# State-space layer: the scan's output copied out of PSUM by ScalarE and multiplied by the gate on GpSimd

## The reference

```python
xz = hidden_states @ in_proj_w.T
x, z = jnp.split(xz, 2, axis=-1)
...
x = silu(jnp.transpose(xc, (0, 2, 1)))          # xc: x after a convolution of 4 taps
A = -jnp.exp(A_log)
dt, Bm, C = jnp.split(x @ x_proj_w.T, [DT_RANK, DT_RANK + D_STATE], axis=-1)
dt = jax.nn.softplus(dt @ dt_proj_w.T + dt_proj_b)
def step(h, ins):
    h = jnp.exp(dt_t[:, :, None] * A) * h + dt_t[:, :, None] * B_t[:, None, :] * x_t[:, :, None]
    y = jnp.einsum('bdn,bn->bd', h, C_t)
    return (h, y)
...
y = jnp.transpose(ys, (1, 0, 2)) + x * D
return y * silu(z) @ out_proj_w.T
```

## Time and profile before

| | |
|---|---|
| median of three executions | 3272.32 us |
| the three | 3270.14, 3272.32, 3275.80 us |
| the profiled execution | 3271.81 us |
| its span in the trace | 3270.1 us |
| mean granted clock of TensorE in the span | 0.919 of full speed |

### The profile page before, as it was taken

How to read it: one execution, slowest core, us unless ns; L and a number is a source line. 1 busy time by engine, 2 the same in 40 slices (tenths; PEclk the granted TensorE clock), 3 DMA queues, 4 the chain that set the end, 5 groups by cost and what they waited for, 6 DMA issues and landing times.

```text
span 3270.1 us, 45199 instructions
## 1 busy us (share of the span) xinstructions
PE 2865.6 (88%) x14018; PEld 1320.2 (40%) x14055; DVE 2167.0 (66%) x3006; ACT 1420.8 (43%) x2463; POOL 1267.8 (39%) x1424
## 2 busy tenths in 40 slices
PE   6895798988988989869999999678899899999986
PEld 5662133333332333236666666563222233223222
DVE  3577876866866767022222222564999999999997
ACT  2341055655655656812122211435445445545442
POOL 1143012112212212210000000744888888898885
PEclk9997588988999989979999999888899999998978
DMA  6166413133132220041111111740000000000000
GB/s 206 52 213 161 152 28 61 28 59 55 34 58 38 51 48 24 19 135 32 32 30 32 32 31 26 224 152 7 1 14 20 1 20 20 1 20 14 1 13 20
DMA packets 175061, 176.60 MB, mean 54 GB/s; under 512 B 50674, under 2 KB 151541, under 8 KB 174749
## 3 DMA queue, kind: packets, MB, share of 16 engines
q1 hardware_dynamic: 168732, 157.52, 18.9%
q0 software_dynamic: 6144, 16.82, 1.6%
HBM read 100.46 MB, written 73.83 MB: 53 GB/s over the span
## 4 chain that ended last, share of the span: by engine, by line
PE 54%; DVE 18%; POOL 10%; issue 9%; ACT 4%; DMA 3%; SPq 1%; POOLq 0%; DVEq 0%; ACTq 0%; PEldq 0%
PE ps L1679 50%; DVE hh L1645 6%; DVE mp L1421 6%; POOL Ch L907 5%; DVE ps L1632 2%; PE ps L1887 2%; POOL yg L806 2%; DMA ks<-qk_parts 1%; ACT Pt L1029 1%; DVE tl L1622 1%; DVE q L1333 1%; SPq L529 1%; PE ps L1843 1%; SPq L620 1%; ACT dA L1209 1%
## 5 line engine op out<-in xcount | busy, mean ns | idle before, releaser
L1421 DVE TENSOR_REDUCE mp<-ps 128x1 f32<-128x1024 f32 (+7 forms) x768 | 669.4, 909 | 245.3 <-PE ps L1679 234.2
L1029 ACT ACTIVATE Pt<-ps 128x512 f32<-128x512 f32 (+3 forms) x1280 | 609.2, 539 | 477.3 <-PE ps L1679 472.2
L907 POOL TENSOR_TENSOR Ch<-hh,Cb 128x1024 f32<-128x1024 f32 x256 | 603.1, 2358 | 41.0 <-DVE hh L1645 41.0
L1679 PE MATMUL ps<-ks,qs 96*128 96x512 bf16 (+3 forms) x1280 | 392.0, 379 | 96.2 <-DVE mp L1421 48.6
L1645 DVE TENSOR_TENSOR_SCAN hh<-dA,hst,ps 128x512 f32<-128x512 f32 x384 | 472.8, 1262 | 0.0
L767 POOL TENSOR_SCALAR_AFFINE_SELECT Pt<-Pt 128x128 f32<-128x128 f32 x512 | 146.8, 292 | 837.1 <-ACT Pt L1029 828.6
L1679 PE MATMUL ps<-qs,ks 99*128 99x512 bf16 (+3 forms) x1280 | 406.9, 365 | 16.0 <-ACT Pt L1029 15.6
L1209 ACT ACTIVATE dA<-ps 128x1024 f32<-128x1024 f32 x256 | 261.8, 1023 | 356.2 <-PE ps L1679 355.8
L1679 PE MATMUL ps<-dtx,pick 32*128 32x512 f32 x1024 | 324.8, 685 | 74.0 <-DVE hh L1645 73.1
L1632 DVE TENSOR_TENSOR ps<-ps,Bb 128x512 f32<-128x512 f32 x512 | 325.4, 680 | 28.0 <-PE ps L1679 27.7
L1679 PE MATMUL ps<-dt,WA 32*128 32x512 f32 x1024 | 321.1, 706 | 15.6 <-ACT dA L1209 14.6
(11 more groups left out here) (303 smaller groups left out, 3770.5 us busy)
## 6 DMA issues: line engine op xcount, KB each, us to landing
W<-in_L_ffn_w SPq DMA_DIRECT2D x16, 1024.0 KB, 12.1
qk_parts<-q SPq DMA_DIRECT2D x32, 384.0 KB, 2.9
qs<-qk_parts SPq DMA_DIRECT2D x96, 128.0 KB, 6.1
ks<-qk_parts SPq DMA_DIRECT2D x96, 128.0 KB, 7.8
expert_out<-yb SPq DMA_DIRECT2D x72, 128.5 KB, 2.6
expert_in<-zero SPq DMA_DIRECT2D x9, 1024.0 KB, 11.5
xg<-expert_in SPq DMA_DIRECT2D x72, 128.0 KB, 2.7
X<-in_L_attn_x SPq DMA_DIRECT2D x4, 1024.0 KB, 9.7
```

Source lines behind the costliest of these rows:

```text
L907: pool.tensor_tensor(Ch[:, k % 6, :, :], hh[:, k % HRING, :, :], Cb[:, par:par + 1, :].broadcast_to([P, 2, CH]), ALU.mult).then_inc(s_Ch, 1)
L1029: act.activation(Pt[:, n % PRING, q0:CH], ps[:, 4 + n % SRING, q0:CH], ACT.Exp, scale=SCALE).then_inc(s_exp, 1)
L1421: dve.tensor_reduce(mp[:, qc, h, t % TPC, k0 // 1024:k0 // 1024 + 1], slot[:, 0:n], AX.X, ALU.max).then_inc(s_free, 1)
L1679: return pe.matmul(o, lhsT, rhs, start=start, stop=stop, **kw)
```

## The change

`gate_y` leaves VectorE. ScalarE gets `take_y`, which copies bank 6 into a new SBUF tile `yv` (one buffer of 128 x 512), at units 10, 18 and 26 and at unit 2 of the next chunk, right behind that unit's `decay`. GpSimd gets `gate_y`, which multiplies `yv` by `zs` into `zs`, at units 11, 19 and 26 and at unit 2 of the next chunk, right behind that unit's `Ch`. `reduce` of the next block now waits for the copy (`s_yev`) and not for the gate, and `take_y` waits for the gate before it, since `yv` has one buffer. The last block's pair stands behind the loop.

```diff
--- before.py
+++ after.py
@@ -402,6 +402,7 @@
         hh = sb("hh", [P, HRING, 2, CH])
         Ch = sb("Ch", [P, 6, 2, CH])
         ob = sb("ob", [P, 2, CH])
+        yv = sb("yv", [P, CH])
         xo = sb("xo", [P, TPC, D])
 
         s_phase = sem("s_phase")
...
@@ -875,6 +876,12 @@
                 pool.wait_ge(s_xs, m + 1)
                 pool.tensor_tensor(dtx[:, par, d, :], dt[:, par, d, :], xs[:, par, d, :], ALU.mult).then_inc(s_dtx, 1)
 
+            def gate_y(n, d):
+
+                pool.wait_ge(s_yev, n * KI + d + 1)
+                pool.wait_ge(s_zs, n + 1)
+                pool.tensor_tensor(zs[:, n % 2, d, :], yv[:, :], zs[:, n % 2, d, :], ALU.mult).then_inc(s_yz, 1)
+
             def add(n, a):
 
                 pool.wait_ge(s_jfree, JOB[f"o{a}", n] + 1)
@@ -914,8 +921,13 @@
                     series(n + 1, 2, 0)
                 if n and u in (1, 3, 5):
                     series(n, (2, 3, 3)[u // 2], (1, 0, 1)[u // 2])
+                if u in (11, 19, 26):
+                    gate_y(n, (11, 19, 26).index(u))
+                if n and u == 2:
+                    gate_y(n - 1, KI - 1)
                 if n and u in (17, 30):
                     add(n - 1, u // 30)
+            gate_y(NC - 1, KI - 1)
             add(NC - 1, 0)
             add(NC - 1, 1)
             stage_end(pool, 6)
@@ -1200,6 +1212,12 @@
                 if n:
                     act.wait_ge(s_sum, 2 * n + a - 1)
                 act.activation(ob[:, a, :], ps[:, BANK[f"o{a}", n], :], ACT.Copy).then_inc(s_jfree, 1)
+
+            def take_y(n, d):
+                act.wait_ge(s_red, (n * KI + d) * 4 + 4)
+                if n or d:
+                    act.wait_ge(s_yz, n * KI + d)
+                act.activation(yv[:, :], ps[:, 6, :], ACT.Copy).then_inc(s_yev, 1)
 
             def decay(k):
 
@@ -1230,6 +1248,10 @@
                 n, u = divmod(k, UNITS)
                 if k + ARING < NC * UNITS:
                     decay(k + ARING)
+                if u in (10, 18, 26):
+                    take_y(n, u // 8 - 1)
+                if n and u == 2:
+                    take_y(n - 1, KI - 1)
                 if n and u in (15, 27):
                     take_o(n - 1, u // 27)
                 if n == 0 and u in (3, 7, 11):
@@ -1260,6 +1282,7 @@
                     take_z(n + 1, u - 28)
                 if u == 31:
                     silu_z(n + 1)
+            take_y(NC - 1, KI - 1)
             take_o(NC - 1, 0)
             take_o(NC - 1, 1)
             stage_end(act, 6)
@@ -1647,12 +1670,6 @@
                 if a:
                     ins.then_inc(s_h, 1)
 
-            def gate_y(n, d):
-
-                dve.wait_ge(s_red, (n * KI + d) * 4 + 4)
-                dve.wait_ge(s_zs, n + 1)
-                dve.tensor_tensor(zs[:, n % 2, d, :], ps[:, 6, :], zs[:, n % 2, d, :], ALU.mult).then_inc(s_yz, 1)
-
             select(0, 0)
             for k in range(NC * UNITS):
                 n, u = divmod(k, UNITS)
@@ -1664,12 +1681,7 @@
                     select(n + 1, 0)
                 if n and u in (0, 4, 8):
                     select(n, u // 4 + 1)
-                if u in (11, 19, 27):
-                    gate_y(n, u // 8 - 1)
-                if n and u == 3:
-                    gate_y(n - 1, KI - 1)
                 scan(k, 1)
-            gate_y(NC - 1, KI - 1)
             stage_end(dve, 6)
 
 
@@ -2064,8 +2076,9 @@
             def reduce(p):
 
                 n, par, d, i, hf = unit_of(2 * p)
+                if i == 0 and p:
+                    pe.wait_ge(s_yev, p // 4)
                 if i == 0:
-                    pe.wait_ge(s_yz, p // 4)
                     mm(ps[:, 6, :], Dd[:, d, :], xs[:, par, d, :], True, False)
                 pe.wait_ge(s_Ch, 2 * p + 2)
                 for j in range(4):
```

More of the change, by code:

```diff
@@ L446, in build @@
         s_jfull, s_jfree = sem("s_jfull"), sem("s_jfree")
-        s_xs, s_zs, s_ln, s_poly, s_mask, s_sel, s_dt, s_dtx = (sem(n) for n in ("s_xs", "s_zs", "s_ln", "s_poly", "s_mask", "s_sel", "s_dt", "s_dtx"))
+        s_xs, s_zs, s_ln, s_poly, s_mask, s_sel, s_dt, s_dtx, s_yev = (sem(n) for n in ("s_xs", "s_zs", "s_ln", "s_poly", "s_mask", "s_sel", "s_dt", "s_dtx", "s_yev"))
         s_dtb, s_dxb, s_dA, s_Bu, s_h, s_hst, s_Ch, s_red, s_yz, s_sum = (sem(n) for n in ("s_dtb", "s_dxb", "s_dA", "s_Bu", "s_h", "s_hst", "s_Ch", "s_red", "s_yz", "s_sum"))
```

## The result

The changed kernel takes 3282.2 us in the median of 15 executions (3272.95 to 3287.21), the kernel before 3272.32 us (15 executions). The ratio is 1.0031, with a 95% interval of 1.0023 to 1.0039: 9.9 us slower, 10 us by the ratio. The forecast was 3280, slower.

What follows compares the result with a forecast made beforehand. VectorE, 97% busy in the state-space loop, was taken as full, with GpSimd lacking slack at some chunk boundaries. 16.3 lost, 9.9 gained and 1.3 lost in the tail gave 7.7 us longer: 3280 us, range 3258 to 3295.

Steps and rivals of the forecast that it cites:

- Direction and place: Whole program: 7.7 us longer, with loss at chunk boundaries and in the tail, gain at units 11 and 19.
- The signs named: GpSimd waits before unit 26's gate, some 20 us; VectorE's mask wait grows 5.7 to some 30; TensorE's waits move under 7.7.
- The late copy: Unit 26: GpSimd stands waiting for ScalarE's queued copy, delaying its later work by 0.9 to 5.1 us at seven boundaries.
- The boundaries: Seven chunk boundaries: GpSimd's delay plus 1.22 us, less slack, makes masks and selects late, 16.3 us lost together.
- The port: Selects on VectorE beside GpSimd's instructions: taken as 0 us longer, with 32 us as the far bound.
- Rival (f): Selects lengthened by the port: half of the 32 us on top of the sum, 3296 us; chance 0.05.
- Units 11 and 19: Inside chunks, GpSimd has room; VectorE gains 0.58 us each, 9.9 us with the last chunk's unit 27.
- The tail: Behind the loop, copy, GpSimd multiplication and one more handover replace the last gate: 1.3 us lost.
- the sum of 7.7 us: Whole program: 16.3 lost at boundaries, 9.9 gained, 1.3 lost in the tail, so 7.7 us longer.
- (b): Loop: GpSimd's 134 free us swallow all and VectorE gains, 16.7 us after the tail: 3256 us; chance 0.13.
- (d): TensorE catches up while VectorE waits, mostly beside unit 27; some 10 us come back: 3270 us; chance 0.16.
- (e): Boundaries have no slack anywhere, as late masks hold ScalarE and its decay: 24.3 us longer, 3297 us; chance 0.12.

Runs made afterwards that it cites:

- e2: Against the kernel before, only the gates of blocks 2 and 3 (units 26 and 2, and the tail's) move to GpSimd: 1.0090, 29.9 us slower.
- e1: Against the kernel before, only the gates of blocks 0 and 1 (units 11 and 19) move to GpSimd: 0.9944, 18.6 us faster.
- e10: The changed kernel timed again on another chip, against the kernel before: 1.0012.
- e3: The changed kernel with ScalarE's copy of block 2 issued at unit 25, ahead of take_dt: 0.9973 against the kernel before, 9.0 us faster.
- e4: All gates on GpSimd, those of blocks 2 and 3 at the next chunk's units 11 and 12, with the earlier copy: 0.9942 against the kernel before.
- e9: e7 plus GpSimd waiting at unit 26 for ScalarE's copy, multiplying nothing; gates on VectorE: 1.0016 against the kernel before.
- e6: The kernel before plus an unused 128x512 multiplication on GpSimd at units 11 and 19: 0.9986, 4.6 us faster.
- e5: The kernel before plus an unused 128x512 multiplication on GpSimd at units 26 and 2: 1.0010, 3 us slower.
- e7: The kernel before plus unused 128x512 copies on ScalarE at units 10, 18, 26 and the next chunk's unit 2: 1.0010.
- e8: e4 with the very last gate done by VectorE straight from PSUM: 0.9919 against the kernel before, 26.9 us faster.

## Why the prediction was right, step by step

**Direction and place: right, shown.** The loss sits at units 26 to 8, in the half that e2 moves, and the gain in the half that e1 moves. The selects wait longer in the one and not in the other. That the chain is GpSimd's series, ScalarE's mask, VectorE's select is shown by the rows above.

**The signs named: kept.** GpSimd waits for the copy at unit 26 (at six boundaries of seven), the selects wait longer, and in this trace VectorE's wait for TensorE moved by 4.2 us in the loop, less than the 7.7 at stake; in e10's it moved by more.

**The late copy: right, and its size right only in sum.** At 1-2 I had GpSimd standing 2.9 us and it was 5.2; at 0-1 2.7 and it was none; at 3-4 some 1.3 and it was 4.1; in all it was 24.0 us, and the same reading of the trace before had given 21.4. That the sum came out is in part luck. At 1-2 VectorE itself waits 2.96 us for TensorE beside it, which it did not before. e3 shows that this step decides the sign: with the copy early 9 us faster, with it late 4 to 10 us slower.

**The boundaries: undersized.** From unit 24 of a chunk to unit 9 of the next the seven came to -1.6, 7.1, 1.8, 5.7, 3.7, 2.5 and 2.4 us against before, 21.6 in all, where I had 16.3. The excess is at the three that had no slack: 16.5 us against 9.5. Two things are in it: the longer stand at unit 26 and the selects.

**The port: the term that failed.** I took 0 for longer selects; they are 8 us longer in all. The Trainium skill's rule (SBUF — State Buffer, "Who interferes with whom"), that one of the two engines waits for the other's whole instruction, fits: in this trace all selects but the first begin while GpSimd has an instruction under way, and each ends 0.6 us behind the end of that instruction. So its length is set by when it starts. A select that has to wait for its mask often starts just after `series` ends, where a product of 2.36 us has begun on GpSimd: the seven of unit 8 take 2.1 to 2.3 us (the one at 2539.41 is among them), and took 2.2 to 2.7 before. After the change nine of the fourteen at units 0 and 4 take 2.1 to 2.3 us too, where three took about as long before, and these two units make up 7.1 of the 8 us. The moved gate itself was the instruction under way for six selects of unit 28; these take 7.8 us where they took 6.0. So the longer selects come mostly from when the select starts and only in a small part from the gate: e1 and e4, with 16 and 32 gates on GpSimd at other units, have shorter ones than before (45.3 and 46.0 us), and e9, with no gate there, has 61.4 us. Rival (f) had the right mechanism at twice the size (16 us), and the term left out cost 8.

**Units 11 and 19: right at seven chunks, undersized at chunk 0.** Between units 9 and 24 chunks 1 to 7 became 10.2 us shorter in all, 1.2 us each in most cases (two gates, as priced), 2.4 and 1.7 in chunks 1 and 4. Chunk 0 became 6.2 us shorter, 62.6 to 56.4. This is so in all kernels that move blocks 0 and 1 (56.3 to 56.4 on three chips) and in none that doesn't, except e6 (57.3). Two parts of it can be read. The select of unit 13 and the product beside it, in the timeline of the kernel before:

```profile
2308.63 2.34 POOL L907 TENSOR_TENSOR Ch<-hh,Cb 128x1024 f32<-128x1024 f32 x1
...
2308.96 2.60 DVE L1622 COPY_PREDICATED tl<-te,dtx 128x512 f32<-128x512 int32 x1
```

and in that of the kernel after, where it starts ahead of the gate on GpSimd and that is the one to be stretched (1.74 and not 1.27 us):

```profile
2307.30 0.81 DVE L1645 COPY_PREDICATED tl<-te,dtx 128x512 f32<-128x512 int32 x1
...
2307.45 1.74 POOL L883 TENSOR_TENSOR zs<-yv,zs 128x512 f32<-128x512 f32 x1
```

That is 1.8 us. Further, between units 9 and 24 TensorE's granted clock was at its lower level (half of full) for 17.1 us before, in two stretches of 3.4 and 13.7, and for 6.8 us after, and VectorE's waits there fell from 4.3 to 1.6 us: 2.7 us. The same 17.1 us stand in the traces of e2, e5, e7 and e9, the same 6.8 in those of e1, e3, e4, e8 and e10, and 10.2 us in that of e6. That the clock is the cause was not tried.

**The tail: right in kind.** 1.3 predicted; from the end of the last `reduce` to the output it is 2.15 us and was 0.91, 1.2 us more. The lower clock, in that `reduce` and in the output's multiplications, took the other 1.5 us, and no term stood for it.

**So the sum of 7.7 us against 6.1 in the traced span and 10 in the medians hides errors that cancelled, which is luck:** the boundaries lost 21.6 and not 16.3, the stretches off the boundaries won 17.0 and not 9.9 (chunk 0 alone 6.2 and not 1.2), the tail lost 2.7 and not 1.3, and the loop began 1.1 us earlier. Of the rivals, (b) is excluded by the result, and load as such by e2 and e4 together. (d) did not show in the first chip's trace, where VectorE's wait for TensorE in the loop went from 21.6 to 17.4 us; in e10's it is 7.2, and the loss is 4 us, so there (d) may be part of the account. (e) is what happened to the slack, but not to its price.

**Open.** Why e1 wins 4 us more and e2 loses 13 us more than the steps give. One rival was not tried: in the traces TensorE is at its lower clock for 160 us of the loop before, 140 in e1, 177 in e2, 133 in e3 and 123 in e4, so of these five the kernels that gained more had less of it. But the changed kernel in e10 has 124 us of it too, and is no gain. Whether it is a cause of the gain or follows from it, these runs don't tell.

## What to carry to other kernels

An engine that is 85% busy can be full for 50 us at a stretch, here at three of seven turns of the loop: before moving work to it, cut its time into the stretches between the points where another engine waits for it, and price the work by the slack of that stretch. A moved instruction that waits on a third engine brings that engine's queue with it; where it stands in both orders was worth 13 to 19 us here (e3), about as much as VectorE spent on all the gates in the loop (18.0 us).

## What the runs showed of the hardware

COPY_PREDICATED of 128x512 with all operands in SBUF took 0.70 to 3.00 us, according to what GpSimd was doing when it started. With nothing under way there it took 0.70 to 0.76 us. Otherwise it ended 0.58 to 0.73 us behind the end of GpSimd's instruction, in all twelve traces and with one exception (the 3.00 us, in e5). The gate's multiplication on VectorE, with one operand in PSUM (0.66 us), never varied by more than 0.04 us. TensorE's lower clock fell differently in kernels that differ little: between units 9 and 24 of chunk 0 there were 17.1 us of it in five traces, 6.8 in six and 10.2 in one. Two chips ran the stages ahead of the state-space layer some 50 us slower than the first; the changed kernel's chunk loop was 989.2 us long on one of them and 999.1 on the first.
